# Queries, keys and values first in every step, the residual behind the softmax's normalisation, the diffusion one step behind its scaling

## The reference, cut to what matters

```python
lap_x = yp_x[:, :, :-2] - 2.0 * y + yp_x[:, :, 2:]          # neighbours within a row
lap_y = yp_y[:, :-2, :] - 2.0 * y + yp_y[:, 2:, :]          # neighbours across positions
du = zX * lap_x + zY * lap_y + zR * y * (1.0 - y)           # the diffusion
hn = layernorm(du); q, k, v = split(hn @ in_proj_w.T + in_proj_b)
probs = softmax(causal(q k^T / sqrt(16)))                   # 16 heads, over the 16 tokens
x1 = du + (probs @ v) @ out_proj_w.T + out_proj_b           # the residual
hn2 = layernorm(x1); logits = hn2 @ router_w.T              # 8 experts, the best two
y = sum over the two: gate * (gelu(hn2 @ w1[e]) @ w2[e])
return x + x1 + y
```

## Time and profile before

| | |
|---|---|
| median of 3 runs | 738.69 us (736.26 to 738.71) |
| the profiled execution | 738.08 us, its span 736.3 us |
| PE busy | 610.8 us (83%) |
| POOL busy | 465.0 us (63%) |
| DVE busy | 429.7 us (58%) |
| ACT busy | 348.7 us (47%) |
| granted TensorE clock over the span | 0.902 of full speed |

### The profile page before, as it was taken

How to read it: one execution, slowest core, us unless ns; L and a number is a source line. 1 busy time by engine, 2 the same in 40 slices (tenths; PEclk the granted TensorE clock), 3 DMA queues, 4 the chain that set the end, 5 groups by cost and what they waited for, 6 DMA issues and landing times. The chain is left out here.

```text
span 736.3 us, 10160 instructions
## 1 busy us (share of the span) xinstructions
PE 610.8 (83%) x2640; PEld 401.8 (55%) x2640; DVE 429.7 (58%) x1028; ACT 348.7 (47%) x814; POOL 465.0 (63%) x562
## 2 busy tenths in 40 slices
PE   2677889683776978869989799999699999999992
PEld 1233444443444655646656557667476767666661
DVE  1256568883999988863895697989943100111110
ACT  4334442421433645436776355666356555444440
POOL 5776567788678762775678885584365853443442
PEclk9688887966788997989999789999989999999998
DMA  4366654123212320342323422243234644444332
GB/s 124 122 212 196 208 170 114 44 82 97 48 44 59 74 60 13 81 95 42 65 40 83 106 30 31 45 88 66 43 76 69 127 85 66 66 66 73 61 56 25
DMA packets 51547, 59.83 MB, mean 81 GB/s; under 512 B 7386, under 2 KB 47075, under 8 KB 51428
## 3 DMA queue, kind: packets, MB, share of 16 engines
q0 software_dynamic: 18288, 23.28, 19.8%
q1 hardware_dynamic: 33204, 35.91, 17.2%
HBM read 35.89 MB, written 27.46 MB: 86 GB/s over the span
## 5 line engine op out<-in xcount | busy, mean ns | idle before, releaser
L979 PE MATMUL b_y<-w_s,hm_hmT 128*128 x568 | 135.6, 382 | 11.1 <-ACT y L548 10.3
L446 POOL DMA_INDIRECT out_dram<-y,xin x71 | 117.1, 1650 | 34.2 <-issue 29.7
L964 PE MATMUL b_h<-w_s,xT 128*128 x284 | 135.0, 598 | 1.6 <-ACT xT L509 1.6
L979 PEld LDWEIGHTS b_y<-w_s,hm_hmT 128*128 128x128 f32 x568 | 102.8, 191 | 25.0 <-issue 13.9
L1056 PE MATMUL b_qk<-wqkv,hT 128*128 128x512 f32 x128 | 94.1, 876 | 0.0
L910 DVE TENSOR_TENSOR pv_prod<-kv,pr 128x1024 f32<-128x1024 f32 (+2 forms) x80 | 82.4, 1072 | 20.0 <-PE b_at L1100 19.9
L681 DVE TENSOR_SCALAR y<-b_y,xin,live 128x256 f32<-128x256 f32 x24 | 13.1, 544 | 137.2 <-PE b_y L979 137.2
L844 DVE TENSOR_TENSOR qk_prod<-q,kv 128x1024 f32<-128x1024 f32 (+2 forms) x80 | 88.2, 1126 | 7.8 <-ACT kv L578 6.9
L1100 PE MATMUL b_at<-ident,pv_prod 128*128 128x128 f32 x544 | 74.5, 287 | 18.4 <-DVE pv_prod L910 17.4
L414 POOL DMA_INDIRECT xs_d<-ring,slot_row x64 | 72.7, 1136 | 19.1 <-issue 18.2
L852 DVE TENSOR_REDUCE sc<-qk_prod 128x64 f32<-128x1024 f32 (+2 forms) x80 | 82.1, 1051 | 0.3
(11 more groups left out here) (166 smaller groups left out, 1019.8 us busy)
## 6 DMA issues: line engine op xcount, KB each, us to landing
xin<-xs_d SPq DMA_DIRECT2D x71, 132.5 KB
w_s<-in_L_ffn_w_dram SPq DMA_DIRECT2D x16, 512.0 KB, 4.4
xp<-in_x_dram SPq DMA_DIRECT2D x32, 128.0 KB
xud<-in_x_dram SPq DMA_DIRECT2D x32, 128.0 KB
out_dram<-x POOLq DMA_DIRECT2D x32, 128.0 KB, 3.3
xud<-in_x_dram SPq DMA_DIRECT2D x32, 126.0 KB
out_dram<-y,xin POOLq DMA_INDIRECT x71
xud<-in_x_dram SPq DMA_DIRECT2D x64, 1.0 KB
```

The lines of the kernel that those rows point to most:

```text
L446: pool.indirect_dma_start(out_rows, bass.IndirectOffsetOnAxis(ap=xin[:, j % NX, H:H + 1].bitcast(U32), axis=0), y[:, j % NY, :], None, com ...
L964: mm = pe.matmul(b_h[:, :], xT[:, k * P:(k + 1) * P], w1_s[:, bass.ds(e * (HC * F) + k * F, F)], start=(k == 0), stop=(k == HC - 1))
L979: mm = pe.matmul(b_y[:, 0:H], hmT[:, k * P:(k + 1) * P], w2_s[:, bass.ds(e * (FC * H) + k * H, H)], start=(k == 0), stop=(k == FC - 1))
```

## The change

PE computes the queries, keys and values of g+1 first in every step except step 20. Behind them come the first slot, the transposes of `hn`, then the projection, and then the transposes of `ring`, which stood first in the step. DVE normalises `ring` behind the products of queries and keys, and adds the residual, with its statistics, behind the normalisation of the softmax of g-1; the second layer norm's variance is aggregated behind the first piece of the value products. POOL and ACT work one step further ahead on the input: ACT scales g+6, POOL makes the sums of g+6, and POOL's diffusion of g+5 comes ahead of them in the step, one step behind its scaling. For that `du` gets a ninth buffer and `ring` gives one up.

```diff
-    RING = 16
+    RING = 15
-    DU = 8
+    DU = 9
         def projected_late(g):
-            return g > AGAIN
+            return g != AGAIN
@@ SP
-                if 2 <= g + AHEAD + 1 < G:
-                    load(g + AHEAD + 1)
+                if 2 <= g + AHEAD + 2 < G:
+                    load(g + AHEAD + 2)
@@ POOL
             neighbours(0)
+            diffuse(0)
+            later_constants()
+            neighbours(1)
             for g in range(-AHEAD, G + 3):
                 adds = [j - 1 for j in done_in(g - 1)]
                 for j in adds[:1]:
                     add_y(j)
                 scatter_at(g, 0)
-                if g == -AHEAD:
-                    diffuse(0)
-                    later_constants()
+                if g + AHEAD + 1 < G:
+                    diffuse(g + AHEAD + 1)
                 if g < 0 <= g + 3:
                     deviation(g + 3, 0)
-                if g + AHEAD + 1 < G:
-                    neighbours(g + AHEAD + 1)
+                if g + AHEAD + 2 < G:
+                    neighbours(g + AHEAD + 2)
                 if 0 <= g < G - 3:
                     deviation(g + 3, 0)
                 if 0 <= g - 2 < G:
                     deviation(g - 2, 1)
                     add_x1(g - 2)
-                if g + AHEAD + 1 < G:
-                    diffuse(g + AHEAD + 1)
@@ ACT
-                if g - 3 >= 0:
-                    ...
-                    affine(flat(h2T), b_tr, 1).then_inc(s["h2T_sb"], 1)
                 if g == -AHEAD:
                     scale(0)
                     setup()
+                    scale(1)
...
                     affine(flat(hT), b_tr, 0).then_inc(s["hT_sb"], 1)
-                if g + AHEAD + 1 < G:
-                    scale(g + AHEAD + 1)
+                if g - 3 >= 0:
+                    ...
+                    affine(flat(h2T), b_tr, 1).then_inc(s["h2T_sb"], 1)
+                if g + AHEAD + 2 < G:
+                    scale(g + AHEAD + 2)
@@ DVE
-                if 0 <= g - 3 < G:
-                    unit(x1[:, (g - 3) % 4, :], g - 3, 1)
...
                     add_up(NPIECE[g] - 1)
+                if 0 <= g - 3 < G:
+                    unit(x1[:, (g - 3) % 4, :], g - 3, 1)
...
+                def residual():
                     dve.wait_ge(s["o_ready"], g - 1)
...
                     total = tick(dve.tensor_tensor(prv, prv, spread(small[:, 32:32 + NH], NH, T), ALU.mult))
                     if ordered:
                         last = top_index(ordered)
+                    st = residual() if g - 2 >= 0 else None
...
                     for m in range(NPIECE[v]):
                         value_products(m)
+                        if m == 0 and st:
+                            aggregate2(st)
@@ PE
-                if g - 3 >= 0:
-                    pe.wait_ge(s["xhat2"], g - 2)
-                    ...
-                if projected_late(g) and 0 <= g + 1 < G:
-                    queries_keys_values(g + 1)
-                if 0 <= g - 2 < G:
+                late = projected_late(g)
+                if not late and 0 <= g - 2 < G:
                     project(g - 2)
-                if not projected_late(g) and 0 <= g + 1 < G:
+                if 0 <= g + 1 < G:
                     queries_keys_values(g + 1)
                 place(g, 0)
                 if 0 <= g + 2 < G:
                     ...
                     mm.then_inc(s["hT_ready"], 1)
+                if late and 0 <= g - 2 < G:
+                    project(g - 2)
+                if g - 3 >= 0:
+                    pe.wait_ge(s["xhat2"], g - 2)
+                    ...
+                    mm.then_inc(s["h2T_ready"], 1)
                 place(g, 1)
```

51 lines of the change are left out of this document (22 added, 29 removed).

## The result

The changed kernel takes **754.57 us** (median of 4 runs, 753.09 to 755.57), the kernel before on the same chip 737.86 (736.26 to 738.71): ratio 1.0223, interval 1.0181 to 1.0265. It is slower by 2.2%, where 734 us was forecast, and outside the range of 721 to 749. The profiled execution has a span of 752.0 us, 15.7 longer, and PE, DVE and POOL are busy 615.0, 438.2 and 457.4 us (before 610.8, 429.7, 465.0): what came on top is waiting and a slower clock, not work.

A forecast was written before the change was run, and what follows sets the result against it. The binding engine was taken to change by stage: a latency loop, POOL, DVE and PE by turns, then PE nearly full. Terms -2.5 - 1 - 2 + 0.7 = -4.8 on 738.08, plus 0.6, gave 734 us; range 721 to 749.

The forecast's parts named there:

- left slots: Slots left over, from 560.3 us in the kernel before: not touched by the change, only their beginning can move.
- Start and steps 3 to 8: First queries 4.9 us later, +1.2 us left by step 3; then six steps of 9.9 for 10.35 us, -2.4.
- The rival that expected the full clock in this loop: Steps 3 to 8 keep the full clock (-10) and PE's waits at 277 and 534 go whole: 722 us, chance 0.16.
- Steps 9 to 13: POOL's 4.44 us wait for ACT's scaling goes; step 13 begins 2.5 us earlier, start and steps 3 to 8 included.
- all of the 4.44 turns into that wait: Bound of 0 gain for steps 9 to 13: POOL waits for DVE's statistics instead of ACT's scaling.
- The rival of the diffusion's company: Steps 9 to 13: diffusions meeting DVE idle or in sums run faster, bound -9 instead of -2.5: 727 us, chance 0.09.
- Steps 16 to 20: PE's 5.21 us wait for ring moves, about 4 us at the new place; 5.49 us copy wait unchanged: -1 us.
- Steps 21 to 27: PE waits about 2 us for step 21's first value piece; some 4 us of ring waits go: -2 us.
- Steps 28 to the end: Slot 28 fills the 5.37 us before ring; residual statistics come 2 to 3 us later: net +0.7, bounds -6 and +10.
- the slower rival: Steps 27 to 31: chain from statistics over add to PE's turn of a tile sets the pace, +14: 748 us, chance 0.22.
- The sign named: Forecast is wrong if PE's waits for value pieces or loads exceed 10 us from 337 us on.

The follow-up runs named there:

- two parts alone: before_ring_behind and before_late_all, each one part of the change alone in the kernel before: ratios 1.0253 and 1.0324.
- before_diff: Kernel before with only the diffusion part of the change (scaling, sums, loads two steps ahead, diffusion first in POOL's step): 739.81 us, ratio 0.9994.
- after_proj_early: Changed kernel with the projection of g-2 straight behind the queries of g+1, ahead of the first slot: 739.62 us, ratio 1.0006.
- the further key and value place: One more place for keys and values, ring cut to 13 buffers: 730.00 us on the kernel before, 743.55 on the changed kernel.
- after_kv21: Changed kernel with one more place for keys and values, ring cut to 13 buffers: 743.55 us, ratio 1.0034.
- after_adds_first: Changed kernel with POOL's second add of a step ahead of the second layer norm's deviation and add_x1: 752.31 us, ratio 1.0204.
- after_slots_behind: Changed kernel with both slots of a two-slot step behind hn, projection and ring: 767.72 us, ratio 1.0391.
- after_early_from21: Changed kernel with the projection straight behind the queries from step 21 on only: 741.29 us, ratio 1.0051.
- early_kv21: Changed kernel with the projection straight behind the queries and one more key and value place (ring 13): 727.01 us, ratio 0.9862.
- after_pieces_first: Changed kernel with DVE's residual and its statistics behind the first two value pieces, projection still late: 731.82 us, ratio 0.9894.
- early_kv21_hn: early_kv21 with the transposes of hn and ACT's copy of them ahead of the first slot: 718.38 us, ratio 0.9732.
- before_ring_behind: Kernel before with only ring moved: normalised behind the products on DVE, transposed behind hn on PE: 758.76 us, ratio 1.0253.
- before_late_all: Kernel before with only the queries ahead of the projection also in the steps up to 19: 762.69 us, ratio 1.0324.

## Why the prediction was wrong

The step that failed is the price of the projection behind a slot. The prediction put it at nothing in steps 16 to 20 and at one wait of about 2 us in steps 21 to 27. Moving that one call back is worth 15 us (754.57 to 739.62), some 13 of them behind step 20, where a wait also costs the slow stretch of PE's clock behind it. What is left of the change is then worth nothing (ratio 1.0006), where -4.8 us had been summed.

By its own steps, on the grid of the table above, us:

| term | forecast | measured |
|---|---|---|
| start to step 9 | +1.2 - 2.4 | -4.8 |
| steps 9 to 12, with 13 to 16 | -1.3 | +4.0 and +1.3 |
| steps 17 to 20 | -1 | +8.1 |
| steps 21 to 26 | -2 | +2.0 |
| step 27 to the left slots | +0.7 | +3.5 |
| left slots | 0 | +1.5 |

The measured terms add up to the 15.7 us of the span within rounding.

**Start and steps 3 to 8: right in kind.** The first `hn` came at 25.85 (forecast about 25.8), the queries of steps 3 to 9 are 7.9 to 10.1 us apart (forecast 9 to 10.6), and the cost of the start was gone by step 9. Counted by DVE's `hn`, step 9 begins 0.4 us earlier (116.1 to 115.7), by the queries 4.8; the forecast of 1.2 lies between. The six steps themselves were shortened about twice as much as forecast, 4.8 us by the queries and 5.2 by `hn`, where the sum has 2.4. That it would come out so only with all parts together wasn't seen: two parts alone lose over 15 us here. The rival that expected the full clock in this loop was wrong, 0.88 for 0.83.

**Steps 9 to 13: the wait changed hands and took the gain.** The bound named was right in kind: "all of the 4.44 turns into that wait". POOL waits 3.72 and 1.97 us for the second layer norm's statistics and, which the prediction did not have, 6.00 us for the first's; all its waits for DVE's statistics from step 9 to 13 are 12.5 us, where it waited 7.3 for ACT before. Step 13 begins at 184.3 instead of 182.9, not at 180. The rival of the diffusion's company got its mechanism and nothing else: three diffusions ran at 0.65 to 0.75 us an operation, where those of the earlier trace rows took up to 1.80 and 2.52, and POOL's busy time from step 9 to 13 fell from 52.7 to 48.5 us, which came back as waiting. The rule of the Trainium skill (SBUF — State Buffer, "Who interferes with whom") thus agrees with the trace, 0.72 beside an idle DVE and 1.80 beside its products, and changes nothing in the time. The diffusion's part alone did gain here, 3.1 us from step 9 to 12 in before_diff; it is the changed kernel that loses 4.0, and with the projection early these are gone (39.4 us for 43.5).

**Steps 16 to 20: a wait priced, what stands behind it not.** I gave PE the queries and a slot to do ahead of `ring`, by which it "stands about 4 us at the new place. Its value pieces then end where they ended. -1 us". PE stood 6.42 us, and the value pieces did not end where they ended: in step 19 they stand behind the residual, this behind the projection, and this now behind a slot that itself waited 4.84 us for ACT. DVE was idle 5.36 us at 317.92, and PE stood 6.93 us for the copy into the values. Of this last wait the text said: "it is released by step 20's second value piece as before: 0", without asking when that piece would now be made. The lateness of the projection is in these rows, but it isn't what makes the stretch longer: in after_proj_early, without DVE's wait in front of the residual, PE stands 6.41 us for `ring` and 7.19 for that copy, and the stretch is as long (97.3 us). What does take it down is the further key and value place, to within 1.8 us of the kernel before with the same place.

**Steps 21 to 27: the term that was mis-sized.** I wrote that "the projection comes behind that slot and PE then waits about 2 us for the first value piece", for step 21 alone, and the wait of 1.97 us at 364.23 is just that. But it is not one wait in one step. Between the queries of steps 21 and 27 the early projection saves 6.8 us, and not as waiting. Of the kernel before, of the changed kernel, then of after_proj_early, the stretch between the same queries:

```profile
343.90:443.30 99.40, 89.42 (x401) 59.72 (x400) 75.53 (x178) 61.07 (x140) 76.83 (x84) 0.93 0.33 66
```

```profile
352.60:454.00 101.40, 92.49 (x401) 61.05 (x400) 69.13 (x171) 59.86 (x136) 66.47 (x77) 0.92 0.28 56
```

```profile
348.70:443.30 94.60, 85.79 (x402) 56.64 (x401) 73.05 (x173) 60.60 (x136) 68.50 (x77) 1.00 0.31 61
```

PE is idle 8.9 us in the changed kernel (101.40 - 92.49) and 8.8 in after_proj_early, and busy 6.7 us longer with the same matmuls (401 and 402 records): all of it is the clock. The same split says what the change did to the kernel before: of the idle time that was to go, 10.0 us, only 1.1 went, and 3.1 us of slower work came on top, for PE had a slow stretch there too, about a wait of 3.22 us, but a shorter one.

What differs is how the idle time is cut up. The changed kernel has waits of 1.97, 2.85 and 1.56 us in this stretch, for value pieces and a load; the longest in after_proj_early is this one:

```profile
359.11 0.41 PE L1086 MATMUL b_tr<-ident,ring 128*128 128x128 f32 x2 [0.99 <-ACT hT L509]
```

By the windows of the changed kernel around the wait of 1.97 us:

```profile
352.60:362.00 9.40, 9.40 (x38) 5.92 (x37) 0.91 (x6) 7.31 (x15) 1.70 (x4) 1.00 0.20 58
362.00:368.00 6.00, 4.03 (x19) 3.05 (x18) 5.82 (x14) 3.14 (x8) 3.35 (x5) 0.71 0.20 22
368.00:374.00 6.00, 6.00 (x15) 2.73 (x16) 4.46 (x13) 3.79 (x9) 4.76 (x9) 0.72 0.45 91
```

PE was full and at full clock (2.4 GHz), then stood 1.97 us, and in that window and the next, 12 us together, the clock is 0.71 and 0.72: 1.2 GHz for over half of the time. Three more kernels with the late projection and the same waits of 1.97 and 1.56 us have a clock of 0.92 to 0.95 in this stretch (after_kv21, after_adds_first, after_slots_behind) and take 100.4 to 101.8 us; after_early_from21 and early_kv21, with the early one, have 1.00 and take 95.0 and 94.6. In after_pieces_first, without that wait, the stretch between the same queries keeps the full clock:

```profile
342.80:432.40 89.60, 85.00 (x402) 56.80 (x401) 69.60 (x171) 59.51 (x136) 62.52 (x76) 1.00 0.31 63
```

The Trainium skill (TensorE: Matmul & The Clock Gate, "HAM oscillation — how this bites in real kernels") has this pattern of a wait that is paid again as a slow stretch behind it, there for DMA waits of about 3 to 5 us; the trace agrees in kind, with shorter waits, 1.97 us here. My sum priced a wait at its length here, though it had priced the clock in steps 3 to 8.

**Steps 28 to the end: the slower rival, named for the wrong reason.** The turns of tiles waited 0.61, 2.87 and 3.75 us for their loads, and one at 411.34, in step 24, 2.85, as forecast. My rival made this chain the price of 14 us and gave 748, near the result; after_adds_first takes it away and gains nothing, and after_pieces_first keeps it (19.2 us) and is 22.7 us faster. So the rival was right on the sign and wrong on the cause. The sign named, "PE's waits for value pieces or for loads add up to over 10 us from 337 us on", did come true: 5.5 us for pieces and 10.1 for those four loads. That the measured time lies near this rival's 748 us is luck.

What stays open: why steps 17 to 20 cost 8.1 us. Some 3.3 of them are PE's busy time, with 14 more matmuls inside these borders and a clock of 0.86 for 0.90, and no single part was shown to be the cause of the rest. With the further place these 8.1 shrink to 1.8 and the loss shows up behind step 27 instead, by 7.9 us, which nobody took apart. And after_pieces_first gains 22.7 us, more than the 15 of the early projection: by the table it has 4 us over it in steps 3 to 8 and 5 in steps 21 to 26, and gives 3.5 back behind them. Since the same edit gave nothing on early_kv21_hn, the surplus isn't the pieces' place by itself; what it is was not settled.

## What to carry to other kernels

When an instruction is moved behind something late, price what stands behind it in its queue, not the instruction itself: the residual was 0.42 us long and held up value products that were ready. The cure can be a swap with its neighbours on the waiting engine (22.7 us here) as well as an undoing of the move (15). And a wait on TensorE costs its length and, where the clock falls behind it, as it did here about a wait of 1.97 us (0.71 and 0.72 from 362 to 374 us), the slow stretch as well: look at busy time at an equal number of matmuls before looking for idle time.

## What the hardware showed that was not expected

The same four matmuls of 512 columns took 3.78 us at 79.70 and 1.99 us at 89.48 in the changed kernel, one step apart:

```profile
79.70 3.78 PE L1058 MATMUL b_qk<-wqkv,hT 128*128 128x512 f32 x4
...
89.48 1.99 PE L1058 MATMUL b_qk<-wqkv,hT 128*128 128x512 f32 x4
```

In a loop whose steps last 8 to 10 us, with one longer pause of PE in each, of 0.75 to 1.81 us, the clock thus goes up and down from step to step. And orders that differ by one move fall from 0.83 to 0.70 and 0.74 in it (before_ring_behind, whose pauses are none longer than 1.59 us, and before_late_all, with six of 2.15 to 3.07), where PE was busy 63.2 and 58.6 us instead of 51.7, with 183 and 173 matmuls for 184: of the 17.1 and 15.6 us that these two lost there, 11.5 and 6.9 are PE's work at the lower clock, and only the rest is waiting.
